# A graph layer on one core: twelve groups of sender rows in another place, four record groups, ten groups of receiver rows ahead

## The reference

```python
dst, src = (edge_index[0], edge_index[1])
edge_feat = jnp.concatenate([h[dst], h[src], rel_pos, distance], axis=-1)
x = jax.nn.silu(edge_feat @ W1 + b1)
x = jax.nn.silu(x @ W2 + b2)
scores = (x @ W3 + b3)[:, 0]
...
alpha = exp_scores / (den[dst] + EPS)
msg = h[src] @ Wv * (alpha * node_weight[src])[:, None]
out = jax.ops.segment_sum(msg, dst, num_segments=num_nodes)
return h + out
...
x = _layernorm(x + _L0_gnn_ref(...), axis=-1)
```

## Time and profile before

| what | value |
|---|---|
| runs of the kernel | 1018.76, 1025.85, 1027.38 us; median 1025.85 |
| profiled execution, its own time | 1024.02 us |
| its span in the trace | 1021.9 us |
| POOL busy | 755.6 us, 74% of the span, 790 instructions |
| DVE, PE, ACT busy | 606.3, 584.4, 515.4 us |
| DMA moved | 198.00 MB, mean 194 GB/s |
| mean granted clock of TensorE | 0.72 of full speed |

### The profile page before, as it was taken

One profiled execution on the slowest core, in us unless ns is written; L12 is line 12 of the kernel. 1 busy time (PEld: TensorE's weight loads), 2 busy tenths in 40 slices (PEclk: granted clock), 3 DMA queues, 4 the chain that ended last, 5 costly groups with the idle time before them and its releaser, 6 DMA issues.

```text
span 1021.9 us, 10972 instructions
## 1 busy us (share of the span) xinstructions
PE 584.4 (57%) x2391; PEld 342.2 (33%) x2391; DVE 606.3 (59%) x2374; ACT 515.4 (50%) x1217; POOL 755.6 (74%) x790
## 2 busy tenths in 40 slices
PE   0999988898954455677666666776667640000000
PEld 0544444444422233344344344444434440000000
DVE  7778787688653626897898788774434784000000
ACT  0465554655544666679798778884434332000000
POOL 6767767666777777777777777777777777777775
PEclk9968758775856778778877877787977755555555
DMA  6688889888984867686787867743222112111110
GB/s 202 204 268 294 299 254 320 272 278 284 277 320 161 286 243 282 216 313 238 254 298 240 314 207 281 246 158 86 71 82 70 58 52 70 45 45 46 46 46 27
DMA packets 77913, 198.00 MB, mean 194 GB/s; under 512 B 19007, under 2 KB 49409, under 8 KB 65304
## 3 DMA queue, kind: packets, MB, share of 16 engines
q1 hardware_dynamic: 49560, 134.37, 35.7%
q0 software_dynamic: 28288, 62.93, 21.6%
HBM read 106.64 MB, written 92.16 MB: 195 GB/s over the span
## 4 chain that ended last, share of the span: by engine, by line
DVE 25%; PE 19%; POOL 17%; issue 15%; DMA 3%; ACT 3%; POOLq 0%; SPq 0%; DVEq 0%; ACTq 0%
POOL out_rows L417 14%; DVE dst L884 5%; PE bank L621 5%; DVE m_q L958 4%; PE bank L608 4%; PE bank L615 4%; POOL hk L413 3%; DMA xin<-in_x 3%; PE bank L598 3%; PE bank L623 2%; DVE est L972 2%; ACT xin L469 2%; DVE hk L967 2%; DVE xin L899 1%; DVE drs L867 1%
## 5 line engine op out<-in xcount | busy, mean ns | idle before, releaser
L469 ACT ACTIVATE xin<-xin,drs 128x128 f32<-128x128 f32 x637 | 258.4, 485 | 74.0 <-DVE drs L869 74.0
L413 POOL DMA_INDIRECT region<-in_xw,snd_t x196 | 188.9, 964 | 77.9 <-issue 46.3
L417 POOL DMA_INDIRECT out_rows<-hk,sidx_t x196 | 191.8, 979 | 59.8 <-issue 58.8
L413 POOL DMA_INDIRECT region<-rec_d,id_t x196 | 186.7, 953 | 59.7 <-issue 59.7
L413 POOL DMA_INDIRECT hk<-in_x,kg_t x196 | 185.9, 949 | 59.8 <-issue 59.8
L573 PE MATMUL bank<-wsv,region 128*128 128x256 f32 x392 | 180.9, 553 | 27.8 <-DVE region L922 14.4
L884 DVE BATCH_NORM_STATS2 dst<-xin 128x6 f32<-128x256 f32 x392 | 137.1, 414 | 26.5 <-DMA xin<-in_x 26.1
L598 PE MATMUL bank<-region,m_q 128*128 128x128 f32 x392 | 74.5, 348 | 93.3 <-DVE m_q L958 93.3
L958 DVE TENSOR_SCALAR m_q<-bank,kcol,acol 128x128 f32<-128x128 f32 x196 | 74.0, 403 | 88.2 <-PE bank L637 84.2
L621 PE MATMUL bank<-hkT,w1a 128*128 128x512 f32 x98 | 67.6, 779 | 86.4 <-issue 66.9
L598 PEld LDWEIGHTS bank<-region,m_q 128*128 128x128 f32 x392 | 62.9, 244 | 105.5 <-DVE m_q L958 105.5
(11 more groups left out here) (179 smaller groups left out, 870.1 us busy)
## 6 DMA issues: line engine op xcount, KB each, us to landing
xin<-in_x SPq DMA_DIRECT2D x49, 1024.0 KB, 7.2
out_rows<-xin SPq DMA_DIRECT2D x49, 1024.0 KB, 4.6
rec_d<-region SPq DMA_DIRECT2D x49, 512.0 KB, 6.7
region<-in_xw,snd_t POOLq DMA_INDIRECT x196, 5.8
hk<-in_x,kg_t POOLq DMA_INDIRECT x196, 4.0
region<-rec_d,id_t POOLq DMA_INDIRECT x196, 3.1
out_rows<-hk,sidx_t POOLq DMA_INDIRECT x196, 2.2
ef_d<-hk SPq DMA_DIRECT2D x9, 196.0 KB, 3.4
```

The source lines that it names most:

```text
L413: pool.indirect_dma_start(out=to, out_offset=None, in_=frm, in_offset=bass.IndirectOffsetOnAxis(ap=index, axis=0)).then_inc(done, 16)
L417: pool.indirect_dma_start(out=out, out_offset=bass.IndirectOffsetOnAxis(ap=index, axis=0), in_=frm, in_offset=None, bounds_check=N - 1, oo ...
L469: ins = nc.scalar.activation(xin[:, j % X_RING, n, :], xin[:, j % X_RING, n, :], ACT.Identity, bias=drs[:, j % 2, 1, n:n + 1], scale=drs[: ...
```

## The change

Four things change, all of them places or numbers.

1. The sender ring has twelve groups in place of six. It leaves `region` and takes the last 12 x 4 x 129 columns of `hk`, a little over twelve of its 49 groups. Those columns belong to receiver groups 36 to 48, which POOL gathers after 26 or more groups of records.
2. The ring of record groups `rec` has four groups in place of three, in the space that `hs` leaves in `region`.
3. POOL issues ten groups of `hk` in place of eight before the first `r` group.
4. By the same rule of `pool_plan` there are then `hk` groups for `r` groups 0 to 38 only, and `sc` group 0 comes ahead of `r` group 41, not behind it.

```diff
-HS_RING, EF_RING, REC_RING, R_RING, X_RING = 6, 4, 3, 12, 4
+HS_RING, EF_RING, REC_RING, R_RING, X_RING = 12, 4, 4, 12, 4
...
-LEAD = 8
+LEAD = 10
...
-        hs = part(HS_RING * TPG * XW).rearrange("p (r q w) -> p r q w", r=HS_RING, q=TPG)
         hsT = part(2 * GE).rearrange("p (r e) -> p r e", r=2)
...
         hflat = hk[:].rearrange("p g q h -> p (g q h)")
+        hs = hflat[:, G * GE - HS_RING * TPG * XW:].rearrange("p (r q w) -> p r q w", r=HS_RING, q=TPG)
```

## The result

| | before | changed |
|---|---|---|
| median of six runs each | 1022.83 us (1018.76 to 1027.38) | 1005.97 us (1005.19 to 1010.22) |
| ratio, 95% interval | | 0.984 (0.9816 to 0.9864) |
| profiled execution, its span | 1024.02, 1021.9 us | 1010.22, 1008.4 us |
| POOL busy | 755.6 us | 754.7 us |

The change makes the kernel 1.6% faster. With three more runs of the kernel before, its median is 3 us lower than the one that the prediction started from.

A forecast was written before the change was run, and what follows sets the result against it. POOL's issue of 786 small DMAs was taken to bound the kernel. Terms -15.9 (sender waits) + 2.3 (table) + 0 gave -13.6 us, so 1010.4 profiled and, 1.8 us carried over, 1012.2 us; range 1004 to 1020.

The forecast's parts named there:

- The bound: Whole kernel: POOL's issue of 786 small DMAs, 1010.5 us busy and idle, is its length; only real waits can go.
- Sender ring: POOL's sender gathers in stage one: twelve groups remove all 14 real waits, 15.9 us; bounds 15.9 and 0.
- The table is late next: First receiver gather: it waits for DVE's table until 253.96 us, so 2.3 of the 15.9 us become a wait.
- Ten groups ahead: First record gather: due at 304.1 us, no wait; with eight groups 5.6 us of wait; worth nothing by itself.
- The move, the record ring, the record ring of stage two: Sender rows moved into `hk`'s tail, four record groups, stage two's record gathers: each zero; late stores at most few tenths.
- Scatters earlier: First scatter: due at 705.5 us, 14.4 us after `dense_written`'s 691.1, so no wait; counted as zero.
- The sum: Whole kernel: -15.9 + 2.3 + 0 = -13.6 us, so 1010.4 us for the profiled execution.
- I carry the difference over: Last step: the profiled execution lay 1.8 us under the median of 1025.85, so 1010.4 becomes 1012.2 us.
- The first, late records: End of stage one: records or stores 10 us later delay the first record gather to 309.7; 1018 us; chance 0.14.
- The second, no gain: Before the first scatter: the 15.9 us turn up as other waits; 1025 us; chance 0.06.
- The third, on the slow side: Stage one: gathers take the loads' bandwidth; loads of 8.5 us in place of 7.2 give 1032 us; slower, chance 0.04.
- the prediction's sign: Stage one, one sign of being wrong: a block load at 8 us or more and tables after 256 us.

The follow-up runs named there:

- the eight groups left out: Changed kernel without its last eight scatter groups (32 scatters): 964.24 us in two runs, 43.4 us less than the changed kernel beside it.
- the repetition: The changed kernel, unaltered, measured once more beside three others: 1007.66 us, ratio 0.9858 to the kernel before.
- The run with fourteen groups: Changed kernel with fourteen groups of receiver rows ahead in place of ten: 1010.53 us, ratio 0.9867 to the kernel before.
- the last set: Last four runs, the unaltered changed kernel (1007.66 us) beside three others, with their own runs of the kernel before (median 1022.89 us).
- The run with eight groups: Sender ring of twelve in its new place alone, eight groups ahead and three record groups as in the kernel before: 1014.71 us, ratio 0.9903.
- ten groups alone: Kernel before with only ten groups of receiver rows ahead in place of eight: 1025.06 us, ratio 1.0023.

## Why the prediction was right

The direction, a gain of over 1%, and the mechanism were right. The time, 1012.2 us, was 6.2 us too high against 1005.97, which is inside the range of 1004 to 1020 but only 2 us from its lower end. By its steps:

**The bound.** POOL's issue, 1010.5 us of busy and idle: shown by the eight groups left out, and the table above fits it. (The 1010.5 us also hold the 2.6 us before the first gather, so they begin at about 0.4 us and not at 3; nothing hangs on it.) That the chain that ended last misleads held as well. After the change POOL has again 17% of it. In the run with a ring of nine, which is as fast and has the same order of work, the page's chain reads

```profile
POOL 56%; issue 18%; DVE 4%; PE 4%; DMA 2%; POOLq 1%; ACT 1%; SPq 0%; DVEq 0%
```

and over the fourteen traces POOL's share of this chain goes from 13 to 56%, while POOL is busy for 74 to 75% of the span in each.

**Sender ring.** "None of the 14 real waits is left": in the trace none. The forecast put group 48 at 246.5 us and the end of the gathers at 251.4; they came at 246.96 and 251.89. The experiments add that nine groups do it.

**The table is late next.** Forecast 2.3 us of wait and the first receiver gather at 253.96; in the profiled execution it was 3.65 us and 255.85, since the table came 1.8 us later there, in the repetition 0.11 us and 252.36. This term is not one number. The release took 0.34 us from DVE's end at 255.51, 0.27 was assumed.

**Ten groups ahead.** Forecast 304.1 for the first record gather and no wait; it was 305.80 and none. The valuation with eight groups, 5.6 us of wait, measured 8.6, and 7.1 us between the medians; the direction held, and the cover is thinner than I wrote. In the changed kernel the last store was issued at 295.53 and landed 9.3 us later, at about 304.8, 1.0 us before the gather that needs it. The forecast had 4.4 us of room there, from a store issued at 292.97 and a landing of 6.7. That no wait appeared in this trace is partly luck: had the table come at its forecast time, the gather would have been due at 303.9 by the pace of this trace (1.9 us sooner than 305.80), before the store had landed.

**The move, the record ring, the record ring of stage two.** Counted as nothing. Three record groups measured the same. For the move no run stands alone. That busy time and loads are unchanged speaks for it, and so does the ring of seven, which lies in the new place as well and has most of the old waits back.

**Scatters earlier.** Forecast 705.5, measured 706.61, no wait. The room of 14.4 us was real, since SP was past its stores at 690.49 + 0.25 = 690.74, 15.9 us ahead. The run with fourteen groups shows the gate appear when compute runs later.

**The sum.** 13.6 us was forecast for the profile pair, and 1024.02 - 1010.22 = 13.8 was measured. That this is so close is partly luck: POOL's waits fell by 12.3 us only, and the rest is busy time and the stretch at the end, which the sum did not have. The weakest step is the last one, "I carry the difference over": the 1.8 us by which the profiled execution lay under the median of three. The median of six runs of the kernel before is 1022.83, so that 1.8 should have been -1.2, which is 3.0 us of the 6.2. The other 3.2 us is the size of the gain between the medians: 16.9 us in the runs of the result (1022.83 - 1005.97) and 1022.89 - 1007.66 = 15.2 us in the last set, where 13.6 was taken. The upper bound of this term, 15.9, was nearer. The changed kernel's two traces differ by 3.5 us in the wait for the tables, about as much as this. It would fit if most of its executions met little of this wait, but the executions without a trace don't show it, so the cause of these 3.2 us stays open.

**The rivals.** The first, late records, came halfway in the changed kernel: the last store was issued 2.6 us later than before and took 2.6 us longer to land, 5.2 of the rival's 10 us, and the first record gather just missed it. The run with eight groups meets the same gate, by an earlier gather and a store that lets POOL go 8.8 us after its issue. The second, no gain, is out by its interval. The third, on the slow side, needed block loads of 8.1 us or more in stage one. With the denser POOL their median was 7.1, against 7.2; one took 8.4, over the 8 us of the prediction's sign, but the tables came before 256. The stretch from 48 to 254 us moved 281 GB/s at a DMA share of 0.84, against 280 at 0.83.

```profile
48.00:254.00 206.00, 185.96 (x593) 96.86 (x594) 158.76 (x624) 116.15 (x316) 154.81 (x162) 0.69 0.84 281
```

POOL is busy 154.81 us in this stretch, 144.90 before, with 162 DMAs in place of 152. The Trainium skill's rule that DMAs of all engines share the same engines ("DMA: Bandwidth & Descriptors", section "Issuing engines are not separate DMA queues") is not contradicted; ten gathers of 64 KB more beside loads of 1 MB just don't show. On the Trainium skill's rule on descriptors and DVE's two-port copies ("SBUF — State Buffer", section "SBUF: two separate sides") the runs show only that the change moved nothing: the sender gathers' mean is 966 ns against 964 before, and the receiver gathers' 948 against 949. Whether such copies make the difference of 15 to 18 ns between the two kinds was not tested.

One detail of the text on the kernel before is to be corrected: the early tensors at the front of `hk` reach into its tenth group, not its eighth. All are read for the last time before `tab_ready`, so no number hangs on it.

## What to carry to other kernels

When one engine only issues, add its busy time and its usual gaps. If that is the span, leave some of its work out to see that it sets the end, look for its waits longer than the usual gap, and don't rely on a chain that leads away from it. A deeper ring turns such waits into gain only up to the next event that the stream needs, so write down for every fixed event (a table, a last store, a flag) when it comes and when the stream will now ask for it; an edit that puts other work in between, worthless alone, may be half of the gain. And a gain taken from one trace is that execution's: state it against that execution, and give the term that depends on a race between two engines as a range.

## What the runs showed that I had not expected

The stretch behind POOL's last DMA depends on how many it issued. With 786 DMAs the span ends 8.0 to 8.4 us after the last one. Without 32 scatters it ends 961.5 - 956.0 = 5.5 us after it:

```profile
955.05 0.97 POOL L418 DMA_INDIRECT out_rows<-xin,fixi  x1 [0.30 <-issue]
```

That is 2.5 us less than in the changed kernel beside it (8.0), for 32 DMAs less, on top of their issue. Most of this stretch is one DRAIN instruction on POOL, which the views don't count as busy. By the trace's records it takes 3.82 us here, 6.76 in the kernel before and in the ring alone, and 6.44 in the other eleven traces, the changed kernel's among them. The last difference also sets those two apart in the sum of all runs (250.4 against 250.0 to 250.2). One run shows the DRAIN shorter with fewer DMAs; why it is 0.3 us longer in two traces was not tested.

The pace of stage one differs between executions of the same plan: the last table came between 251.7 and 256.1 us over ten traces (before, changed twice, ring alone, ten groups alone, three record groups, fourteen groups, rings of nine and seven, and the run with fewer scatters), though the kernel's other engines do the same work in each up to there.

The last record store's time to land differs as much. It lands between 5.4 us (ring of nine) and 9.3 us (changed, first trace) after its issue, in the eight traces that record it, while the median of all 49 stores of a trace is 3.0 to 6.7. A gate that hangs on one transfer is not priced by the median of its kind.
